# Mamba block: POOL works one state further ahead over four buffers, and weighs five of sixteen states

## The reference

```python
def _mamba(x, inW, convW, convb, xprojW, dtW, dtb, A_log, Dskip, outW):
    xz = jnp.einsum('bld,ed->ble', x, inW)
    xs, z = jnp.split(xz, 2, axis=-1)
    ...   # causal convolution over 4 positions, per channel
    xs = jax.nn.silu(jnp.transpose(xc + convb[None, :, None], (0, 2, 1)))
    xdb = jnp.einsum('bld,ed->ble', xs, xprojW)
    dt, Bm, Cm = jnp.split(xdb, [DT_RANK, DT_RANK + D_STATE], axis=-1)
    dt = jax.nn.softplus(jnp.einsum('blr,dr->bld', dt, dtW) + dtb)
    dA = jnp.exp(dt[..., None] * A)
    dBx = dt[..., None] * Bm[:, :, None, :] * xs[..., None]
    def step(h, inputs):
        dA_t, dBx_t, C_t = inputs
        h = h * dA_t + dBx_t
        y = jnp.einsum('bds,bs->bd', h, C_t)
        return (h, y)
    ...   # scan over the positions
    y = (y + xs * Dskip) * jax.nn.silu(z)
    return jnp.einsum('bld,ed->ble', y, outW)
```

## Time and profile before

| | |
|---|---|
| runs shown | 2932.03, 2926.57, 2915.05 us; median 2926.57 us |
| profiled execution | 2937.55 us, span 2935.8 us |
| busy over the span | PE 2069.2 us (70%), DVE 1920.8 (65%), ACT 1440.0 (49%), POOL 1328.1 (45%) |
| granted TensorE clock | 0.854 of full speed over the span |
| state loop of the Mamba stage | 127 to 1110 us of the span, a third of it |

### The profile page before, as it was taken

One profiled execution on the slowest core, in us unless ns is written; L12 is line 12 of the kernel. 1 busy time (PEld: TensorE's weight loads), 2 busy tenths in 40 slices (PEclk: granted clock), 3 DMA queues, 4 the chain that ended last, 5 costly groups with the idle time before them and its releaser, 6 DMA issues. The chain is left out here.

```text
span 2935.8 us, 35273 instructions
## 1 busy us (share of the span) xinstructions
PE 2069.2 (70%) x10366; PEld 1059.0 (36%) x10366; DVE 1920.8 (65%) x2484; ACT 1440.0 (49%) x2523; POOL 1328.1 (45%) x974
## 2 busy tenths in 40 slices
PE   2687786877868668648543888863068888888876
PEld 1233233332323224316332666651024444444312
DVE  6289989899898994772255777753176555555541
ACT  1476766767667643414423343322125646556453
POOL 2288788887888870040013666616401111101253
PEclk9899999999999997779766898866559989999875
DMA  1344444444545440001300000003222131313111
GB/s 35 90 142 131 136 143 138 145 125 142 143 134 143 129 132 8 1 22 43 92 0 0 0 0 0 0 8 81 76 71 82 51 97 51 94 48 85 30 29 49
DMA packets 146984, 214.72 MB, mean 73 GB/s; under 512 B 30746, under 2 KB 58292, under 8 KB 146228
## 3 DMA queue, kind: packets, MB, share of 16 engines
q1 hardware_dynamic: 142756, 204.72, 23.9%
q0 software_dynamic: 4096, 8.40, 1.4%
HBM read 193.91 MB, written 23.86 MB: 74 GB/s over the span
## 5 line engine op out<-in xcount | busy, mean ns | idle before, releaser
L505 PE MATMUL ps<-m_hC,ident 128*128 128x512 f32 x1024 | 527.9, 648 | 206.7 <-POOL m_hC L710 104.4
L700 POOL TENSOR_TENSOR m_dBx<-m_du,m_rowB 128x1024 f32<-128x1024 f32 x256 | 602.4, 2384 | 0.1
L2317 ACT ACTIVATE a_pT<-ps 128x512 f32<-128x512 f32 (+2 forms) x640 | 319.6, 553 | 400.9 <-PE ps L2182 397.4
L2367 DVE TENSOR_REDUCE a_mx<-ps 128x2 f32<-128x1024 f32 (+2 forms) x320 | 349.2, 1116 | 169.1 <-PE ps L2160 128.9
L626 ACT ACTIVATE ps<-m_delta,m_A 128x512 f32<-128x512 f32 x512 | 341.3, 686 | 154.3 <-DVE m_h L774 153.3
L505 PEld LDWEIGHTS ps<-m_hC,ident 128*128 128x128 f32 x1024 | 190.2, 199 | 517.8 <-DVE m_hC L783 194.8
L774 DVE TENSOR_TENSOR_SCAN m_h<-ps,m_carry,m_dBx 128x512 f32<-128x512 f32 x256 | 311.3, 1265 | 28.9 <-POOL m_dBx L700 28.9
L774 DVE TENSOR_TENSOR_SCAN m_h<-ps,m_dBx 128x512 f32<-128x512 f32 x256 | 295.2, 1205 | 47.0 <-ACT ps L626 24.2
L2497 POOL TENSOR_SCALAR_AFFINE_SELECT a_pT<-a_pT 128x512 f32<-128x512 f32 x128 | 81.5, 637 | 526.3 <-ACT a_pT L2317 525.6
L783 DVE TENSOR_TENSOR m_hC<-m_h,ps 128x1024 f32<-128x1024 f32 x192 | 234.1, 1219 | 15.1 <-issue 1.3
L710 POOL TENSOR_TENSOR m_hC<-m_h,m_rowC 128x1024 f32<-128x1024 f32 x64 | 155.8, 2435 | 187.3 <-DVE m_h L774 187.3
(11 more groups left out here) (361 smaller groups left out, 3932.2 us busy)
## 6 DMA issues: line engine op xcount, KB each, us to landing
m_rowB<-bc_rows SPq DMA_DIRECT2D x256, 256.0 KB, 3.9
m_rowC<-bc_rows SPq DMA_DIRECT2D x256, 256.0 KB, 3.9
a_w<-in_L3f_w1T SPq DMA_DIRECT2D x39, 256.0 KB, 2.6
a_w<-in_L3f_w2T SPq DMA_DIRECT2D x39, 256.0 KB, 3.3
qk_parts<-p_part SPq DMA_DIRECT2D x24, 256.0 KB
expert_rows<-in_zero_rows SPq DMA_DIRECT2D x39, 128.0 KB, 2.7
a_xs<-expert_rows SPq DMA_DIRECT2D x39, 128.0 KB, 2.1
expert_out<-a_y SPq DMA_DIRECT2D x39, 128.0 KB, 3.2
```

Of the source, the lines that this page charges most:

```text
L505: mm = pe.matmul(ps[:, bankY + c, :], k.ident[:], hC[:, n % 3, c, :], start=False, stop=n % NS == NS - 1)
L700: pool.tensor_tensor(dBx[:, n % 3], du[:, i % 2, :, chunk(i, x)], rowB[:, n % 4, :].unsqueeze(1).to_broadcast([P, HALF, CH]), ALU.mult).th ...
L2317: act.activation(dst, src, ACT.Exp).then_inc(t_read, 1)
L2367: dve.tensor_reduce(mx[:, c % 2, :, es[0]:es[0] + len(es), t, x // CH], src, AX_X, ALU.max)\
```

## The change

Five things are edited, all in `mamba_stage`. `POOL_STATES` becomes (1, 4, 6, 9, 12). The rings `dBx`, `h` and `hC` get four buffers each, and every wait on them is written with `NBUF`. To make room, the weights `inx` and `outw`, which only the setup reads, lie in the last buffer of `hC`. POOL's weighing comes one product later: product(n), then weigh(n - 2). TensorE sums a POOL state behind the state that follows it, and `sums_to` says which count of `summed` frees a buffer. On DVE the residual moves from q = 3 and 23 to 4 and 24, and the gate moves behind the weighing of the next chunk's state 0.

```diff
-POOL_STATES = (1, 5, 9, 13)
+POOL_STATES = (1, 4, 6, 9, 12)
+NBUF = 4
...
-        dBx, h, hC = (sb(x, [P, 3, HALF, CH]) for x in ("dBx", "h", "hC"))
+        dBx, h, hC = (sb(x, [P, NBUF, HALF, CH]) for x in ("dBx", "h", "hC"))
+        inx, outw = (hC[:, NBUF - 1, c, :].rearrange("p (d n) -> p d n", d=2) for c in range(HALF))
...
+        def sums_to(n):
+            s = n % NS
+            return n + 1 + (s in POOL_STATES) - (s - 1 in POOL_STATES)
...                                  # TensorE
-                    add_up(n)
+                    if s not in POOL_STATES:
+                        add_up(n)
+                    if s - 1 in POOL_STATES:
+                        add_up(n - 1)
...                                  # POOL, product(n)
-                    if n >= 3:
-                        pool.wait_ge(scanned, (n - 2) * HALF)
+                    if n >= NBUF:
+                        pool.wait_ge(scanned, (n - NBUF + 1) * HALF)
...                                  # POOL, weigh(n); the same on DVE
-                        if n >= 3:
-                            pool.wait_ge(summed, n - 2)
+                        if n >= NBUF:
+                            pool.wait_ge(summed, sums_to(n - NBUF))
...                                  # POOL, order
                     product(n)
-                    if n > 0:
-                        weigh(n - 1)
+                    if n > 1:
+                        weigh(n - 2)
...                                  # DVE, scan(n)
-                    if n >= 3:
-                        dve.wait_ge(*weighed(n - 3))
-                        j, y, t = parts(n - 3)
+                    if n >= NBUF:
+                        dve.wait_ge(*weighed(n - NBUF))
+                        j, y, t = parts(n - NBUF)
...                                  # DVE, order
                     scan(n)
-                    if s == 0 and n > 0:
-                        gate(*parts(n - 1)[0:2])
-                    if q == 3 and i > 0:
+                    if q == 4 and i > 0:
                         residual(i - 1, 1)
-                    if q == 23:
+                    if q == 24:
                         residual(i, 0)
                     if q in (25, 26) and i + 1 < N:
                         add_soft(i + 1, q - 25)
                     if s not in POOL_STATES:
                         weigh(n)
+                    if s == 0 and n > 0:
+                        gate(*parts(n - 1)[0:2])
```

More of the change, by code:

```diff
@@ L331, in mamba_stage @@
         An = sb("A", [P, 2, HALF, NS])
-        inx, outw, pw = sb("inw_x", [P, 2, DI]), sb("outw", [P, 2, DI]), sb("projw", [P, 2, D])
+        pw = sb("projw", [P, 2, D])
         wc = sb("wc", [P, 2, HALF, D])
@@ L504, in add_up @@
                     for c in range(HALF):
-                        mm = pe.matmul(ps[:, bankY + c, :], k.ident[:], hC[:, n % 3, c, :],
+                        mm = pe.matmul(ps[:, bankY + c, :], k.ident[:], hC[:, n % NBUF, c, :],
                                        start=False, stop=n % NS == NS - 1)
@@ L645, in keep @@
                         end = 0 if ITEMS[i][0] else CH - 1
-                        act.copy(carry[:, s, :], h[:, n % 3, :, end]).then_inc(carried, 1)
+                        act.copy(carry[:, s, :], h[:, n % NBUF, :, end]).then_inc(carried, 1)
                 inputs(0, 0)
@@ L697, in product @@
                     pool.wait_ge(s_B[n % 4], 16 * (n // 4 + 1))
-                    if n >= 3:
-                        pool.wait_ge(scanned, (n - 2) * HALF)
-                    pool.tensor_tensor(dBx[:, n % 3], du[:, i % 2, :, chunk(i, x)],
+                    if n >= NBUF:
+                        pool.wait_ge(scanned, (n - NBUF + 1) * HALF)
+                    pool.tensor_tensor(dBx[:, n % NBUF], du[:, i % 2, :, chunk(i, x)],
                                        rowB[:, n % 4, :].unsqueeze(1).to_broadcast([P, HALF, CH]), ALU.mult).then_inc(dbx, 1)
@@ L707, in weigh @@
                         pool.wait_ge(scanned, (n + 1) * HALF)
-                        if n >= 3:
-                            pool.wait_ge(summed, n - 2)
-                        pool.tensor_tensor(hC[:, n % 3], h[:, n % 3],
+                        if n >= NBUF:
+                            pool.wait_ge(summed, sums_to(n - NBUF))
+                        pool.tensor_tensor(hC[:, n % NBUF], h[:, n % NBUF],
                                            rowC[:, n % 4, :].unsqueeze(1).to_broadcast([P, HALF, CH]),
@@ L723, in _ @@
                         inputs(i + 1, 0)
+                weigh(NST - 2)
             @block.vector
@@ L773, in scan @@
                         first = carry[:, s, c:c + 1] if x else 0.0
-                        dve.tensor_tensor_scan(time(h[:, n % 3, c, :]), time(ps[:, bankA + m % 3, :]),
-                                               time(dBx[:, n % 3, c, :]), first, ALU.mult, ALU.add).then_inc(scanned, 1)
+                        dve.tensor_tensor_scan(time(h[:, n % NBUF, c, :]), time(ps[:, bankA + m % 3, :]),
+                                               time(dBx[:, n % NBUF, c, :]), first, ALU.mult, ALU.add).then_inc(scanned, 1)
                 def weigh(n):
@@ L780, in weigh @@
                     dve.wait_ge(scanned, (n + 1) * HALF)
-                    if n >= 3:
-                        dve.wait_ge(summed, n - 2)
-                    dve.tensor_tensor(hC[:, n % 3], h[:, n % 3],
+                    if n >= NBUF:
+                        dve.wait_ge(summed, sums_to(n - NBUF))
+                    dve.tensor_tensor(hC[:, n % NBUF], h[:, n % NBUF],
                                       ps[:, bankC, :].unsqueeze(1).to_broadcast([P, HALF, CH]), ALU.mult).then_inc(hc_dve, 1)
```

## The result

| | before | after |
|---|---|---|
| median of six runs | 2931.31 us (2915.05 to 2939.93) | 2857.63 us (2845.97 to 2862.31) |
| ratio of the runs, 95% interval | | 0.9739 (0.9714 to 0.9765) |
| profiled execution | 2937.55 us | 2862.31 us, span 2860.6 |
| start of the last residual, the end of the Mamba stage | 1112.14 us | 1042.47 us |

The account below looks back on a forecast made before the run. DVE, busy 884.75 of 983 us, was taken to bound the Mamba state loop, with holes made by POOL's order. Terms -21.6 - 69.5 - 8.4 + 22.4 = -77.1 took 2926.6 to 2850 us; range 2824 to 2898.

Parts of the forecast that it names:

- 16 products off DVE: Mamba state loop: a fifth POOL state takes one product with C per chunk off DVE, -21.6 us.
- holes behind POOL states: DVE's scans: 57 waits caused by POOL weighing before its next dBx product all close, -69.5 us.
- residual's wait: DVE's residual, moved one state later, no longer waits for TensorE's projection, -8.4 us.
- ACT stalls: State loop: ACT's next-item preparation with table loads delays decays, 3.2 us per item, +22.4 us, bounds 0 and twice this.
- It fits by 0.3 us: SyncE's row B load: lands 4.3 us after the weighing, needed within 4.66; counted 0, bounds 0 to 10 us.
- POOL waiting for row B: Sign listed in advance that the prediction is wrong: POOL held up by SyncE's row B loads.
- Shared port: DVE's softplus adds beside POOL: 14 adds take 31.5 us, as before; counted 0, possible 15 us either way.
- A: Rival: no ACT stall in the state loop, the whole 99.5 us comes, 2827 us; chance 18%.
- B: Rival: TensorE's sums end last in first chunks, the gate waits, 31 us back, 2881 us; chance 23%.
- C: Rival: nothing gained, the holes only move from dBx to ACT and the gate, 2927 us; chance 7%.
- D: Rival: POOL becomes the bound, each of 80 weighings still waiting 2.9 us, 3004 us; chance 10%, with anything slower.

Follow-up runs that it names:

- e2: Changed kernel with the four POOL states of before (1, 5, 9, 13) instead of five; ratio 0.9803 to the kernel before, stage end 1059.4 us.
- e3: Changed kernel with gate and residual back at their old places (residual at q = 3 and 23); ratio 0.9755 to the kernel before, stage end 1041.8 us.
- e4: Changed kernel with three buffers instead of four, later weighing kept; ratio 0.9776 to the kernel before, stage end 1053.4 us.
- e11: Changed kernel unedited, measured again; 2869.69 us, ratio 0.9786 to the kernel before, stage end 1043.9 us.
- e6: Changed kernel with POOL states 1, 3, 5, 9, 13 and POOL's du for the second chunk made early, at q = 3; ratio 0.9758 to the kernel before.
- e7: e6 with DVE's second softplus add moved from q = 26 to 29; ratio 0.9754 to the kernel before, stage end 1035.1 us.
- e5: Changed kernel with Relu for Silu and log in the Mamba stage, so ACT loads no tables between decays; ratio 0.9681 to the kernel before.
- e8: Changed kernel with six POOL states (1, 4, 6, 9, 11, 13); ratio 0.9742 to the kernel before, stage end 1039.4 us.
- e1: Kernel before with only the five new POOL states, order and three buffers as before; ratio 1.0135, stage end 1155.1 us.
- e9: Changed kernel with DVE's second softplus add at q = 28 instead of 26; ratio 0.9738 to the kernel before, stage end 1038.0 us.

## Why the prediction was right

| term | forecast | profile |
|---|---|---|
| 16 products off DVE | -21.6 | -20.7 (DVE busy); e2 prices the state at 16.9 with the stalls it brings |
| holes behind POOL states | -69.5 | 69.5 to 0.6 |
| residual's wait | -8.4 | 8.4 to 0, but worth nothing (e3) |
| ACT stalls | +22.4 | +21.1 + 7.2, and 2.3 - 1.3 without a named releaser: +29.3 |
| sum | -77.1 | -68.7 from the waits and DVE's busy time; end of stage -69.7 |

*Holes.* The reading that all 57 were POOL's, the 15 named "ACT" among them, is borne out: one of 0.6 us is left. e4 shows that the new order closes them with three buffers as well. Four buffers in the old order were not run; the earlier trace rows has POOL waiting for nothing but scans ahead of its weighings, so there was no wait that a buffer could take away.

*ACT.* The places were right: 28 scans and 14 products. Here is the chain at q = 7 in the changed kernel, ACT then DVE, beside the earlier trace rows:

```profile
379.48 0.69 ACT L637 ACTIVATE ps<-m_delta,m_A 128x512 f32<-128x512 f32 x1 [1.66 <-DVE m_h L786]
...
384.63 1.30 ACT L637 ACTIVATE ps<-m_delta,m_A 128x512 f32<-128x512 f32 x2
```

```profile
378.22 4.56 DVE L786 TENSOR_TENSOR_SCAN m_h<-ps,m_dBx 128x512 f32<-128x512 f32 x4
383.35 1.22 DVE L795 TENSOR_TENSOR m_hC<-m_h,ps 128x1024 f32<-128x1024 f32 x1 [0.57 <-ACT ps L647]
385.45 2.34 DVE L786 TENSOR_TENSOR_SCAN m_h<-ps,m_dBx 128x512 f32<-128x512 f32 x2 [0.88 <-ACT ps L637]
```

The chain from 379.48 to 385.32 is the 5.84 us of before. It starts 1.26 after scan(6) where I took 1.2, and scan(8) follows 0.13 behind it where I took 0.05; the stall is 1.45 and not 1.2. The four places come to 0.57 + 0.88, 0.90, 0.32 + 0.88 and 0.40 = 3.95 us an item against 3.2. This term was mis-sized by 5 to 7 us: a hand-over from one engine to the other cost 0.06 and 0.13 here, and in a chain that is late every one counts. The opposite mis-sizing did not happen elsewhere, so the forecast was some 7 us too fast for the stage, and the 5.6 us behind the stage, which I had not forecast, covered it. That the total came out at 2850 was luck to that extent; the second measurement (e11, 62 us) lies 15 us from the forecast's 77.

*SyncE.* "It fits by 0.3 us" was wrong. Row B lands in 4.5 us (median) instead of 3.9, and POOL waits for it 13 times, 6.8 us in all. By the prediction's own list, POOL waiting for row B was a sign of being wrong; it came true for this term alone. It cost DVE at most 0.6 us, as POOL was early there.

*Shared port.* Unchanged, as taken: 14 adds in 31.5 us, as in the earlier trace rows.

*Rivals.* A is out: the stalls came. B's mechanism is absent in the changed kernel (the gate waits once, 2.1 us, at the very end, as it did before). But it is near: e2, e6 and e7 have 0.4 us of it at seven of the eight first-chunk gates, e5 and e8 up to 0.9, and e4 meets it through hC. C is out with the 69.7 us, D by e8.

## What to carry to other kernels

When one engine works for another and also consumes that one's output, put its next delivery in front of the consuming instruction; that order closed 69 us of waits here, with three buffers as with four, and moving work without it (e1) made the kernel slower. Before counting a closed wait as a gain, list every chain that ran in its shadow: its length doesn't change, only the time it has, and its stall is the chain plus two hand-overs (0.2 us here) minus that time. A wait that vanishes ahead of a later stall is worth nothing (e3), and a slack read off a trace holds only as long as nobody upstream gets faster (e9).

## What the runs showed of the hardware

The shared port can shut DVE out for longer than one POOL instruction. It was seen once. POOL and DVE in e5, an item in which the first add starts while a POOL product runs (it ends at 884.55):

```profile
884.48 2.38 POOL L721 TENSOR_TENSOR m_hC<-m_h,m_rowC 128x1024 f32<-128x1024 f32 x1
886.77 4.68 POOL L711 TENSOR_TENSOR m_dBx<-m_du,m_rowB 128x1024 f32<-128x1024 f32 x2
892.61 2.35 POOL L700 TENSOR_TENSOR m_du<-m_delta,m_u 128x1024 f32<-128x1024 f32 x1 [1.16 <-DVE m_delta L753]
```

```profile
883.99 8.54 DVE L753 TENSOR_TENSOR m_delta<-m_delta,m_soft 128x1024 f32<-128x1024 f32 x1
```

The add with two SBUF inputs stands from 883.99 to 892.53. Three POOL instructions run back to back in that time at their usual length, and it finishes only when POOL itself waits for it. Wherever else an add met a busy POOL, it got in behind the instruction that was running (1.4 to 3.3 us, against 1.2 alone). The Trainium skill, "SBUF — State Buffer", section "Who interferes with whom", says that the one that issues first holds the pair for its instruction and the other blocks; this run shows that the blocked one need not be next.
